# A state-space layer and a routed feed-forward layer in one kernel: one pass instead of two for the last 42 inner units of the down product

## The chip, the cores and the metric

The kernel runs on one core of a Trainium2 chip. A core has a matrix engine (TensorE, PE in the profile; its weight loads are PEld), VectorE (DVE), ScalarE (ACT), GpSimd (POOL) and SyncE (SP), each with its own stream of instructions, which meet by semaphores. The metric is the time of one execution on the device in microseconds (us).

## What is computed

There are 4096 tokens (2 sequences of 2048) of width 256. First comes a diagonal state-space layer with residual and layer norm, and then a feed-forward layer over the result `x`:

```python
gate = x @ Wg.T + routing_bias                      # 8 experts, the best 4 per token
weights = softmax(gate where chosen) * chosen
out = swiglu(x, Ws1, Ws2, Ws3)                      # the shared expert, every token
for e in 8 experts:                                 # H = 682 inner units
    out += weights[:, e] * swiglu(x, W1[e], W2[e], W3[e])
y = layernorm(x + out)
# swiglu(u, w1, w2, w3) = (silu(u @ w1.T) * (u @ w2.T)) @ w3.T
```

Everything is float32. The products of the feed-forward layer are made in float16 with both factors split into a high and a low half: high x high + high x low + low x high.

## The kernel before

**Stages.** Eight steps of 512 tokens make the state-space layer (0 to 120 us; the first shared block lies among them). Then come shared blocks of 256 tokens each, nine ahead of the experts and seven behind them. Meanwhile GpSimd scatters every token's row to its four experts' places (`scatter`, lines 618 to 627: 4 x 32 indirect DMAs, `pad_rows` after each of the first three). The eight experts run over their rows in full blocks of 256 rows and at most one half block of 128 at an expert's end (`expert_blocks`): here 63 full and 6 half ones. With the 16 shared blocks that makes 79 full and 6 half blocks. At the end the experts' rows are gathered and added (`gather`, line 670), and the last layer norm is made lot by lot in the tail (`finish`, from line 1319, on VectorE, after the low parts of the block that was just run).

**A block.** The 682 inner units are 5 whole chunks of 128 and a last chunk (c = FC = 5) of REM = 42. TensorE makes `up` (line 921: 6 matmuls for each of the 11 column sets, 66 of them) into `psA`. For each chunk ScalarE makes the silu (764), VectorE multiplies (`gated`, 1241), ScalarE rounds to the high half (`high`, 770), and VectorE subtracts for the low half (`low`, 1250). TensorE then makes `down` (lines 944 and 949), chunk by chunk, each after a wait for its low half, and after the last chunk's matmuls the outputs are scaled and stored by ScalarE (796) or added by VectorE (1268). `up` takes the chunks in order too, so silu and the halves of the last chunk lie beside `down` of the first ones.

**The last chunk.** Its high half stands in rows 0 to 41 of `g_hi[:, 5]` and its low half in rows 64 to 105 of the same tile. The high half of the weights stands in both places of `w3[..., 0, ...]`; `w3[..., 1, ...]` has the low half of the weights in rows 0 to 63 and zeros below. Two matmuls over 106 rows for each 128 tokens make all the products (line 949): 4 in a full block, 2 in a half one.

**Weights.** Two sets for the experts lie in `work` (w = e % 2), one for the shared expert in `wshared`. All arrive as float32 in `stage` and are split. The shared set is split by ScalarE and VectorE (`shared_high`, `shared_low`), so is the first expert's (`first_high`, `first_low`), and the other seven by GpSimd: `convert_step` runs `high_part` (553, 554) and `low_part` (560, 563) over six pieces. For experts 1 and 2 these steps stand between the scatters of the second and fourth choice (`convert_beside`); for expert 3 the conversion comes after the last scatter and the pad rows (loop from line 684), and those of the later experts after the end of the expert whose set they take. At the end of a conversion `weight_set_ready` is raised (line 588), for which TensorE waits before each expert (`first` in `experts`).

## Time and profile before

| | us |
|---|---|
| runs shown (3) | 1084.09, 1082.38, 1077.70 |
| median | 1082.38 |
| the profiled execution | 1085.63 |
| its span, first to last instruction | 1083.8 |
| TensorE busy | 1009.8 (93%) |
| VectorE busy | 580.3 (54%) |
| ScalarE busy | 502.7 (46%) |
| GpSimd busy | 533.6 (49%) |
| mean granted clock of TensorE | 0.98 of full speed |

Spans and busy times are of the profiled execution. Busy shares are means over stages: what a stage waits for must be read in its timeline. A matmul's own length in the rows is that of its way through the array, where several are at once, so its price is taken from the distance of blocks. In the timeline, "[idle before <- releaser]" is the time in which the engine stood still before the row, and what ended it.

### The profile page before, as it was taken

To read this page: it belongs to the slowest core of one execution; us is meant where nothing else is said; L and a number is where in the kernel's file an instruction comes from. 1 tells how busy PE (TensorE), PEld (TensorE's weight loads), DVE (VectorE), ACT (ScalarE), POOL (GpSimd) and SP (SyncE) were. 2 spreads that over 40 slices of the span, in tenths; PEclk is the share of its full clock that TensorE was granted. 3 is DMA by queue.
4 is the path that set the end of the run, shared out by engine and by line. 5 is a ranking of instruction groups with operands and counts; after the bars stand their busy time and mean duration, and the time that the engine had idled before them with its cause. 6 is when DMAs were issued, how large, how long until landed. Compare 5 with 4: busy or idle time off the path is not lost.

```text
span 1083.8 us, 27280 instructions
## 1 busy us (share of the span) xinstructions
PE 1009.8 (93%) x8784; PEld 857.8 (79%) x8785; DVE 580.3 (54%) x1584; ACT 502.7 (46%) x1282; POOL 533.6 (49%) x486
## 2 busy tenths in 40 slices
PE   7897989988999999999989999999999999999984
PEld 3455878876888888788878878878888888888864
DVE  3898885545444345644545344444345444344676
ACT  2555554432444444444444444544444444454454
POOL 3465135358233337623664006065678674676761
PEclk9998999998999999999999999999999999999998
DMA  7855223432532333253244223127763764866673
GB/s 223 200 137 117 59 70 96 141 93 75 167 99 86 94 94 99 84 162 95 56 132 126 54 49 112 46 53 163 114 103 62 113 104 79 116 101 99 86 141 103
DMA packets 167716, 113.84 MB, mean 105 GB/s; under 512 B 113388, under 2 KB 159983, under 8 KB 166512
## 3 DMA queue, kind: packets, MB, share of 16 engines
q0 software_dynamic: 30480, 59.41, 25.8%
q1 hardware_dynamic: 114944, 32.33, 14.7%
q10 hardware_dynamic: 22240, 21.50, 5.8%
q8 instruction: 21, 0.34, 0.1%
q14 instruction: 31, 0.25, 0.1%
HBM read 47.09 MB, written 40.96 MB: 81 GB/s over the span
## 4 chain that ended last, share of the span: by engine, by line
PE 69%; DMA 10%; DVE 9%; issue 5%; ACT 4%; POOL 1%; SPq 1%; ACTq 1%; DVEq 0%; POOLq 0%
PE psA L921 44%; PE psB L944 17%; DMA rows_by_place<-y_rows,place 4%; PE psB L949 3%; PE psA L872 3%; DMA y_sum<-rows_by_place,place 2%; DVE g_lo L1250 2%; DVE g L1241 1%; PE psC L903 1%; ACT sil L764 1%; DVE stat L1329 1%; ACT y_sum L836 1%; SPq L465 1%; PE psC L896 1%; DMA xb_odd<-rows_by_place 1%
## 5 line engine op out<-in xcount | busy, mean ns | idle before, releaser
L1241 DVE SCALAR_TENSOR_TENSOR g<-psA,sil 128x256 f32<-128x256 f32 (+1 forms) x510 | 207.7, 413 | 442.7 <-ACT sil L764 405.9
L764 ACT ACTIVATE sil<-psA 128x256 f32<-128x256 f32 (+1 forms) x510 | 187.1, 373 | 299.6 <-PE psA L921 224.0
L670 POOL DMA_INDIRECT y_sum<-rows_by_place,place x128 | 199.5, 1559 | 105.7 <-DMA y_sum<-rows_by_place,place 80.3
L921 PE MATMUL psA<-xb,work 128*128 128x256 f16 x2046 | 233.4, 276 | 8.1 <-issue 4.3
L921 PE MATMUL psA<-xb_odd,work 128*128 128x256 f16 x2112 | 235.9, 273 | 4.5 <-DMA xb_odd<-rows_by_place 3.7
L625 POOL DMA_INDIRECT rows_by_place<-y_rows,place x128 | 128.6, 1005 | 225.9 <-DMA rows_by_place<-y_rows,place 180.9
L944 PE MATMUL psB<-work,g_hi 128*128 128x256 f16 x1320 | 222.3, 273 | 11.8 <-DVE g_lo L1250 11.3
L921 PEld LDWEIGHTS psA<-xb,work 128*128 128x128 f16 x2046 | 201.9, 99 | 35.8 <-issue 10.1
L770 ACT ACTIVATE g_hi<-g 128x256 f16<-128x256 f32 (+1 forms) x510 | 206.3, 405 | 51.4 <-DVE g L1241 44.1
L921 PEld LDWEIGHTS psA<-xb_odd,work 128*128 128x128 f16 x2112 | 205.8, 98 | 30.5 <-issue 6.6
L1250 DVE TENSOR_TENSOR g_lo<-g,g_hi 128x256 f16<-128x256 f32 (+1 forms) x425 | 209.2, 492 | 8.7 <-ACT g_hi L770 2.9
L944 PE MATMUL psB<-work,g_lo 128*128 128x256 f16 x660 | 180.4, 273 | 0.0
L944 PEld LDWEIGHTS psB<-work,g_hi 128*128 128x128 f16 x1320 | 126.4, 98 | 34.0 <-DVE g_lo L1250 19.0
L921 PE MATMUL psA<-xb,wshared 128*128 128x256 f16 x1056 | 121.4, 276 | 4.2 <-DVE g L1241 2.9
L921 PEld LDWEIGHTS psA<-xb,wshared 128*128 128x128 f16 x1056 | 104.0, 99 | 18.8 <-DVE g L1241 4.3
L553 POOL TENSOR_SCALAR work<-stage 128x704 f16<-128x704 f32 (+1 forms) x42 | 36.1, 859 | 119.4 <-PE psB L949 109.6
L944 PEld LDWEIGHTS psB<-work,g_lo 128*128 128x128 f16 x660 | 64.7, 98 | 7.6
L872 PE MATMUL psA<-work,sm 128*128 128x512 f32 x128 | 60.6, 624 | 7.3 <-DMA work<-xT 7.3
L560 POOL TENSOR_TENSOR work<-stage,work 128x704 f16<-128x704 f32 (+2 forms) x42 | 63.2, 1505 | 2.9
L944 PE MATMUL psB<-wshared,g_hi 128*128 128x256 f16 x320 | 54.2, 273 | 8.7 <-DVE g_lo L1250 7.3
L796 ACT ACTIVATE eb<-psB,row_weights_odd 128x256 f32<-128x256 f32 x64 | 26.8, 470 | 74.5 <-PE psB L949 58.5
L796 ACT ACTIVATE eb<-psB,row_weights 128x256 f32<-128x256 f32 x62 | 26.0, 470 | 72.7 <-PE psB L949 54.3
(135 smaller groups left out, 709.8 us busy)
## 6 DMA issues: line engine op xcount, KB each, us to landing
stage<-wpack POOLq DMA_DIRECT2D x9, 2176.0 KB, 9.2
rows_by_place<-eb ACTq DMA_DIRECT2D x63, 256.0 KB
work<-xT SPq DMA_DIRECT2D x8, 512.0 KB, 4.9
work<-half_beta SPq DMA_DIRECT2D x8, 512.0 KB, 4.9
work<-x_tok POOLq DMA_DIRECT2D x8, 512.0 KB, 6.0
out<-y_sum ACTq DMA_DIRECT2D x5, 512.0 KB
rows_by_place<-y_rows,place POOLq DMA_INDIRECT x128, 2.5
y_sum<-rows_by_place,place POOLq DMA_INDIRECT x128
```

The costliest lines, as they stand in the source:

```text
L553: t.add(pool.tensor_scalar(parts_of(w, a, m)[0], stage[:, a:a + m], WS, 1.0, ALU.mult, ALU.mult))
L560: t.add(pool.tensor_tensor(lo[:, 0:full], stage[:, a:a + full], hi[:, 0:full], ALU.subtract))
L625: pool.indirect_dma_start(out=xs, out_offset=bass.IndirectOffsetOnAxis(ap=place[:, k, n:n + 1], axis=0), in_=y_rows[:, n, :], in_offset=No ...
L670: pool.indirect_dma_start(out=y_sum[:, n, :], out_offset=None, in_=xs, in_offset=bass.IndirectOffsetOnAxis(ap=place[:, k, n:n + 1], axis=0 ...
L764: act.activation(sil[r0:r0 + n, c % SLOTS, 0:T], psA[0:n, c % HVS, 0:T], ACT.Silu, scale=1.0 / (XS * WS)).then_inc(silu_ready, 1)
L770: act.activation(g_hi[0:n, c, 0:T], g32[0:n, c % SLOTS, 0:T], ACT.Copy).then_inc(gated_high_ready, 1)
L796: last = act.activation(eb[:, j, :], psB[:, j, 0:D], ACT.Copy, scale=row_weights[slot][:, j, e:e + 1])
L872: last = pe.matmul(psA[:, q, :], wdi[:, w, k, m * P:(m + 1) * P], xt[b][:, k, :], start=(k == 0), stop=(k == KD - 1))
L921: last = pe.matmul(dst, W[:, ws, k, ci, :], xb[slot][:, KD * xs_ + k, 0:T], start=(k == 0 and n == 0), stop=(k == KD - 1 and n == 2))
L944: pe.matmul(o, a[:, c, j * P:(j + 1) * P], W3[:, ws, c, :], start=(c == 0 and n == 0), stop=False)
L1241: dve.scalar_tensor_tensor(g32[0:n, c % SLOTS, 0:T], src, 1.0 / (XS * WS), sil[r0:r0 + n, c % SLOTS, 0:T], ALU.mult, ALU.mult).then_inc(ga ...
L1250: dve.tensor_tensor(dst, g32[0:n, c % SLOTS, 0:T], g_hi[0:n, c, 0:T], ALU.subtract)\
```

## The change

The last chunk's down product takes one pass over 128 rows. The 42 units are two parts: Q = 32 units and QV = 10 units.

- `pack` lays the weights so that the up product itself makes three copies of the last 10 units (rows 32 to 41, 42 to 51, 52 to 61). Silu and multiplication run over 64 rows instead of 42.
- `g_hi[:, 5]` then holds: high of the 32 units in rows 0 to 31, low of the 10 in rows 32 to 41, high of the 10 in rows 42 to 61, low of the 32 in rows 64 to 95 and high of the 32 in rows 96 to 127. For this ScalarE makes a second copy (`high_doubled`) and VectorE makes the low half in two instructions.
- `w3[..., 1, ...]` of that chunk holds the high weights in rows 0 to 51 and 64 to 95 (`MIXED`) and the low ones elsewhere. VectorE makes this by a low part over all rows and two copies (shared set, first set); GpSimd by two multiplications with per-row factors (`low_row`, `low_sign`) ahead of one subtraction.
- Three memsets of GpSimd go, eight small ones of VectorE come at the start.

```diff
+    Q = 32
+    QV = REM - Q
+    MIXED = [(0, Q + 2 * QV), (R2, R2 + Q)]
...
-            pool.memset(w3[SH][:, 1, FC * D:DW], 0.0).then_inc(consts_ready, 1)
...
 def low_part(t, w, a, m):
                 t.add(pool.tensor_tensor(lo[:, 0:full], stage[:, a:a + full], hi[:, 0:full], ALU.subtract))
                 if full < m:
+                    t.add(pool.tensor_scalar(stage[:, a + full:a + m], stage[:, a + full:a + m], low_row[:, 0:1], 1.0,
+                                             ALU.mult, ALU.mult))
+                    t.add(pool.tensor_scalar(lo[:, full:m], hi[:, full:m], low_sign[:, 0:1], 1.0,
+                                             ALU.mult, ALU.mult))
                     t.wait()
-                    t.add(pool.tensor_tensor(lo[0:R2, full:m], stage[0:R2, a + full:a + m], hi[0:R2, full:m],
-                                             ALU.subtract))
+                    t.add(pool.tensor_tensor(lo[:, full:m], stage[:, a + full:a + m], lo[:, full:m], ALU.subtract))
...
-            for w in range(2):
-                pool.memset(w3[w][:, 1, FC * D:DW], 0.0).then_inc(sets_cleared, 1)
-            pool.wait_ge(sets_cleared, 2)
+            pool.sem_inc(sets_free, 1)
+            pool.wait_ge(rows_marked, 8)
...
 def silu(c):
-                    n = P if c < FC else REM
+                    n = P if c < FC else R2
...
 def high(c):
-                    n = P if c < FC else REM
+                    n = P if c < FC else R2
                     act.activation(g_hi[0:n, c, 0:T], g32[0:n, c % SLOTS, 0:T], ACT.Copy).then_inc(gated_high_ready, 1)
+                    if c == FC:
+                        act.activation(g_hi[R2 + Q:P, c, 0:T], g32[0:Q, c % SLOTS, 0:T], ACT.Copy)\
+                            .then_inc(high_doubled, 1)
...
 def down(w, g, T=TB):
                     pe.wait_ge(gated_low_ready, NC * g + c + 1 + SLOTS)
+                    if c == FC:
+                        pe.wait_ge(high_doubled, g + 1)
...
-                            r = R2 + REM
-                            for ws in range(2):
-                                last = pe.matmul(o, g_hi[0:r, c, j * P:(j + 1) * P], W3[0:r, ws, c, :],
-                                                 start=False, stop=(ws == 1))
+                            last = pe.matmul(o, g_hi[:, c, j * P:(j + 1) * P], W3[:, 1, c, :], start=False, stop=True)
...
 def shared_low(i):                                  # first_low(i) likewise
-                dve.scalar_tensor_tensor(lo[:, 0:full], stage[:, a:a + full], WS, hi[:, 0:full],
-                                         ALU.mult, ALU.subtract).then_inc(shared_low_ready, 1)
+                dve.scalar_tensor_tensor(lo, stage[:, a:a + m], WS, hi, ALU.mult, ALU.subtract)\
+                    .then_inc(shared_low_ready, 1)
                 if full < m:
-                    dve.scalar_tensor_tensor(lo[0:R2, full:m], stage[0:R2, a + full:a + m], WS, hi[0:R2, full:m],
-                                             ALU.mult, ALU.subtract).then_inc(shared_low_ready, 1)
+                    dve.wait_ge(shared_low_ready, i + 1)
+                    for r, end in MIXED:
+                        dve.tensor_copy(lo[r:end, full:m], hi[r:end, full:m]).then_inc(shared_low_ready, 1)
...
 def gated(c):
-                    r0, n = (0, P) if c < FC else (R2, REM)
-                    src = psA[:, c % HVS, TB:TB + T] if c < FC else psA[R2:R2 + REM, c % HVS, 0:T]
+                    r0, n = (0, P) if c < FC else (R2, R2)
+                    src = psA[:, c % HVS, TB:TB + T] if c < FC else psA[R2:P, c % HVS, 0:T]
...
 def low(c):
                     if c < FC:
-                        dst, n = g_lo[:, c, 0:T], P
+                        rows = [(g_lo[:, c, 0:T], 0, P)]
                     else:
-                        dst, n = g_hi[R2:R2 + REM, c, 0:T], REM
-                    dve.tensor_tensor(dst, g32[0:n, c % SLOTS, 0:T], g_hi[0:n, c, 0:T], ALU.subtract)\
-                        .then_inc(gated_low_ready, 1)
+                        rows = [(g_hi[R2:R2 + Q, c, 0:T], 0, Q), (g_hi[Q:REM, c, 0:T], Q, REM)]
+                    for dst, r, end in rows:
+                        last = dve.tensor_tensor(dst, g32[r:end, c % SLOTS, 0:T], g_hi[r:end, c, 0:T], ALU.subtract)
+                    last.then_inc(gated_low_ready, 1)
```

## Rows read from the trace of the kernel before

**Rows 1.** The page, part 1: busy us, share, instructions of each engine.

```profile
PE 1009.8 (93%) x8784; PEld 857.8 (79%) x8785; DVE 580.3 (54%) x1584; ACT 502.7 (46%) x1282; POOL 533.6 (49%) x486
```

**Rows 2.** Timeline, undisturbed blocks: start, us, engine, line, operation, [idle before].

```profile
507.34 0.42 ACT L770 ACTIVATE g_hi<-g 42x256 f16<-42x256 f32 x1 [0.21 <-DVE g L1241]
...
507.79 0.42 DVE L1250 TENSOR_TENSOR g_hi<-g,g_hi 42x256 f16<-42x256 f32 x1
...
509.33 0.60 PE L949 MATMUL psB<-work,g_hi 106*128 106x256 f16 x4
...
520.25 0.60 PE L949 MATMUL psB<-work,g_hi 106*128 106x256 f16 x4
```

**Rows 3.** Timeline of GpSimd (POOL), scatters, pad rows and conversion, 145 to 531 us.

```profile
145.72 1.15 POOL L625 DMA_INDIRECT rows_by_place<-y_rows,place  x1 [30.18 <-DVE y_rows L1135]
...
528.92 0.98 POOL L613 DMA_INDIRECT rows_by_place<-zeros,pad_at  x1 [1.91 <-DMA rows_by_place<-zeros,pad_at]
530.51 0.77 POOL L553 TENSOR_SCALAR work<-stage 128x704 f16<-128x704 f32 x1 [0.61 <-issue]
```

**Rows 4.** Timeline of GpSimd: one multiplication, and the ends of three conversions.

```profile
8.94 0.43 POOL L567 TENSOR_SCALAR half_beta<-sm 128x256 f32<-128x256 f32 x1
...
266.74 0.99 POOL L625 DMA_INDIRECT rows_by_place<-y_rows,place  x1 [0.82 <-POOL work L563]
...
451.29 0.74 POOL L563 TENSOR_TENSOR work<-stage,work 64x256 f16<-64x256 f32 x1
452.86 0.99 POOL L625 DMA_INDIRECT rows_by_place<-y_rows,place  x1 [0.82 <-DMA rows_by_place<-y_rows,place]
...
549.99 0.66 POOL L563 TENSOR_TENSOR work<-stage,work 64x256 f16<-64x256 f32 x1
551.27 0.63 POOL L550 DMA_DIRECT2D stage<-wpack  x1 [0.62 <-POOL work L563]
```

**Rows 5.** Timeline of TensorE between experts 2 and 3.

```profile
551.19 0.38 PE L949 MATMUL psB<-work,g_hi 106*128 106x256 f16 x2
552.45 3.77 PE L921 MATMUL psA<-xb_odd,work 128*128 128x256 f16 x33 [0.87 <-DMA xb_odd<-rows_by_place]
```

**Rows 6.** By windows, line 949 alone: us, PE busy (count), PEld, clock, DMA.

```profile
0.00:552.00 552.00, 22.93 (x148) 14.21 (x148) 0.98 0.41 111
552.00:985.00 433.00, 23.29 (x152) 14.04 (x152) 1.00 0.51 97
985.00:1084.00 99.00, 4.21 (x28) 2.71 (x28) 0.96 0.59 105
```

**Rows 7.** Timeline of VectorE and TensorE beside GpSimd's conversions.

```profile
243.44 2.10 DVE L1250 TENSOR_TENSOR g_hi<-g,g_hi 42x256 f16<-42x256 f32 x1
245.60 0.61 PE L949 MATMUL psB<-work,g_hi 106*128 106x256 f16 x4 [1.30 <-DVE g_hi L1250]
...
825.86 0.93 DVE L1250 TENSOR_TENSOR g_hi<-g,g_hi 42x256 f16<-42x256 f32 x1
...
826.85 0.61 PE L949 MATMUL psB<-work,g_hi 106*128 106x256 f16 x4
```

**Rows 8.** Timeline of VectorE at the end of a half block.

```profile
359.75 0.28 DVE L1250 TENSOR_TENSOR g_hi<-g,g_hi 42x128 f16<-42x128 f32 x1
```

**Rows 9.** Timeline of TensorE at 649 us, then all engines' busy by windows.

```profile
649.34 9.04 PE L921 MATMUL psA<-xb,work 128*128 128x256 f16 x66 [2.06 <-issue]
...
649.00:654.00 5.00, 4.66 (x28) 3.56 (x29) 0.42 (x1) 0.47 (x2) 4.83 (x6) 0.66 0.14 32
```

**Rows 10.** Timeline of GpSimd: the first gathers of the third and fourth choice.

```profile
915.00 1.54 POOL L670 DMA_INDIRECT y_sum<-rows_by_place,place  x1 [12.33 <-DMA rows_by_place<-eb]
...
988.65 1.54 POOL L670 DMA_INDIRECT y_sum<-rows_by_place,place  x1 [3.98 <-DMA rows_by_place<-eb]
```

**Rows 11.** Timeline of VectorE in the tail.

```profile
1031.41 0.42 DVE L1250 TENSOR_TENSOR g_hi<-g,g_hi 42x256 f16<-42x256 f32 x1
1031.86 2.06 DVE L1329 BATCH_NORM_STATS2 stat<-y_sum 128x6 f32<-128x256 f32 x6
```

More of the change, by code:

```diff
@@ L143, in build @@
         neg_half = sb("neg_half", [P, JT], F32)
+        low_row = sb("low_row", [P, 1], F32)
+        low_sign = sb("low_sign", [P, 1], F32)
         start_state = sb("start_state", [P, 1], F32)
@@ L267, in build @@
         gated_high_ready = sem("gated_high_ready")
+        high_doubled = sem("high_doubled")
         gated_low_ready = sem("gated_low_ready")
@@ L575, in _ @@
                 if s == len(pieces):
-                    pool.wait_ge(shared_low_ready, len(pieces) + 1)
+                    pool.wait_ge(shared_low_ready, len(pieces) + len(MIXED))
                     fetch(1)
@@ L593, in conversion @@
             def conversion(n):
-                return Tally(pool, convert_steps, 3 * len(pieces) + 1, n - 2)
+                return Tally(pool, convert_steps, 3 * len(pieces) + 3, n - 2)
             def convert(n, w):
@@ L646, in _ @@
             pad_rows(0)
-            pool.wait_ge(first_low_ready, len(pieces) + 1)
+            pool.wait_ge(first_low_ready, len(pieces) + len(MIXED))
             fetch(2)
@@ L986, in _ @@
             pe.wait_ge(states_read, 2 * NSTEP)
-            pe.wait_ge(shared_low_ready, len(pieces) + 1)
+            pe.wait_ge(shared_low_ready, len(pieces) + len(MIXED))
             down(SH, 0)
@@ L994, in _ @@
             pe.wait_ge(blocks_ready, 1)
-            pe.wait_ge(first_low_ready, len(pieces) + 1)
+            pe.wait_ge(first_low_ready, len(pieces) + len(MIXED))
             pe.sem_inc(weight_set_ready, 1)
@@ L1004, in _ @@
         def _(dve):
+            for flag, high in ((low_row, 0.0), (low_sign, -1.0)):
+                dve.memset(flag[:, :], high).then_inc(rows_marked, 1)
+            dve.wait_ge(rows_marked, 2)
+            for flag in (low_row, low_sign):
+                dve.memset(flag[Q:R2, :], 1.0).then_inc(rows_marked, 1)
+                dve.memset(flag[R2 + Q:P, :], 1.0).then_inc(rows_marked, 1)
+            dve.wait_ge(rows_marked, 6)
+            for flag, high in ((low_row, 0.0), (low_sign, -1.0)):
+                dve.memset(flag[Q:Q + 2 * QV, :], high).then_inc(rows_marked, 1)
             dve.wait_ge(small_loaded, 16)
@@ L1401, in pack @@
         up[:, :, :, n:2 * FC:2, :] = wt[..., :FC * P].reshape(E1, P, KD, FC, P)
-        up[:, :, :, 2 * FC, n * 64:n * 64 + REM] = wt[..., FC * P:]
+        up[:, :, :, 2 * FC, n * 64:n * 64 + 32] = wt[..., FC * P:FC * P + 32]
+        for r in range(32, 32 + 3 * (REM - 32), REM - 32):
+            up[:, :, :, 2 * FC, n * 64 + r:n * 64 + r + REM - 32] = wt[..., FC * P + 32:]
     down = np.zeros((E1, P, FC + 1, D), W3.dtype)
@@ L1405, in pack @@
     down[:, :, :FC] = w3t[:, :FC * P].reshape(E1, FC, P, D).transpose(0, 2, 1, 3)
-    for n in range(2):
-        down[:, n * 64:n * 64 + REM, FC] = w3t[:, FC * P:]
+    for r in (0, 64, 96):
+        down[:, r:r + 32, FC] = w3t[:, FC * P:FC * P + 32]
+    for r in range(32, 32 + 3 * (REM - 32), REM - 32):
+        down[:, r:r + REM - 32, FC] = w3t[:, FC * P + 32:]
     wpack = np.concatenate([up.reshape(E1, P, -1), down.reshape(E1, P, -1)], axis=2)
```

16 lines of the change are left out of this document (9 added, 7 removed).

## The prediction

> **What bounds the kernel now.** I read the page's busy shares first: TensorE is busy 93% of the span, so at first sight every matmul taken out is time gained [rows 1]. The timeline of one undisturbed block comes next. The end of one block's down product and the end of the next lie 10.92 us apart (509.33 to 520.25) [rows 2], and a block of 256 rows is 100 matmuls of 256 columns: 66 of the up product, 30 of the whole chunks, 4 of the last chunk. One matmul thus costs 10.92 / 100 = 0.109 us of TensorE. (The mean of 273 ns that the groups show is the pipelined length of one, not its price.) The third view is the timeline of GpSimd, because a kernel that is 93% TensorE can still have points where TensorE waits for somebody who doesn't get faster. There is one. From 145.72 to 528.92 us GpSimd issues the scatters and the pad rows one by one, most of them after the landing of an earlier one, and from 530.51 it converts the weights of expert 3 (the fourth) [rows 3]. That conversion ends at 550.65, GpSimd goes on at 551.27, and TensorE, whose last matmuls of expert 2 begin at 551.19, begins expert 3 at 552.45 [rows 4, 5]. Nothing in that chain of GpSimd waits for TensorE. So TensorE reaches expert 3 less than a microsecond from the moment its weights are ready: the kernel has two bounds until 552 us and mostly one after it.
>
> **What goes.** Line 949 issues 148 matmuls before 552 us, 152 between there and 985, and 28 after it, 328 in all [rows 6]; half of them go, 164 x 0.109 = 17.9 us of TensorE. That is 0.22 us for each of 79 full blocks and 0.11 for each of 6 half blocks. The remaining pass reads 128 rows and not 106, as the 96 other matmuls of a block do at the same 0.109, so that costs nothing.
>
> **What comes, in each block.** VectorE makes the low part of the last chunk in two passes instead of one, 0.42 us more; ScalarE copies 32 rows a second time, again 0.42 us, since a pass over 42 rows takes that [rows 2] and the columns stay. In an undisturbed block both have cover: the low pass ends at 508.21 and TensorE first reads its rows at 509.33 [rows 2], 1.1 us later. The second pass leaves 0.7 us, and the earlier end of the down product doesn't touch that, since the saved matmuls lie behind the read. ScalarE's copy runs beside VectorE's first piece. Behind it are queued the scaling of the output rows and the next block's silu, both later than the down product. These blocks gain the full 0.22 us. If that cover were gone, each would lose 0.42.
>
> Where GpSimd converts weights the cover is gone. The pass that takes 0.42 us takes 2.10 at 243.44, and TensorE waited 1.30 us for it; at 825.86 it takes 0.93 and ends 0.06 us before TensorE's matmul [rows 7]. There the new pass is on the path. Its cost lies between 0.42 and 2.10 less the 0.22 gained. I take 0.43, the undisturbed row, since two GpSimd passes seldom hit both pieces. From expert 3 on I count five such blocks (ending at 574, 662, 725, 816 and 827), before it some eight.
>
> The rule here is that VectorE and GpSimd hold a port against each other. The Trainium skill, SBUF — State Buffer, "Who interferes with whom", says that a VectorE instruction with two inputs in SBUF contends with a GpSimd instruction that reads SBUF and that the loser waits for the whole instruction. The added low piece is such an instruction, so by that page it could wait a full GpSimd pass each time; by that rule alone the five blocks would cost what the second rival below gives. The rows agree that the same pass can be 0.42 or 2.10 us.
>
> In a half block the low passes are the path: the last takes 0.28 us and TensorE's two matmuls follow at its end [rows 8]. One more pass, 0.28, less one matmul, 0.11: 0.17 us lost in each.
>
> **What comes on GpSimd.** Each of seven conversions loses a pass over 64 rows x 256 columns and gets one over 128 rows (equal, 0.66 to 0.74 us) and two multiplications of 256 columns. Such a multiplication took 0.43 us at 8.94 [rows 4]. Two are 0.86; I take 0.8, as they follow one another, with 0.6 and 1.1 as ends. The three memsets that leave GpSimd lay at the start and ahead of a wait of 30.18 us [rows 3]: nothing. The eight small memsets of VectorE lie before its first work, nothing either. For the shared set and the first set the low part becomes one longer pass and two copies, a few tenths beside work that waits for TensorE; I take none, with 0.4 as the end.
>
> **How that chain moves.** The scatters' start comes after the ranks, which VectorE counts right after block 1's low passes: one pass more, 0.42, less the 0.22 that TensorE gave in block 0: +0.2 us. The conversion for expert 1 ends with a scatter that waited for the conversion's own last pass, so +0.8 passes on whole; that for expert 2 ends with one that waited for a landing, 0.82 us after the pass, so between 0 and +0.8, I take 0.7, as the hand-over after the pass costs up to 0.6 (551.27 is that far behind 550.65) [rows 4]. The conversion for expert 3 adds 0.8 in full. Together the weights are ready 2.5 us later. Before, TensorE's start lay up to 0.9 us behind the release (of its 0.87 us of idle I can't tell how much is branching) [rows 5]. So expert 3 starts 1.6 us **later**, ends 0.5 and 2.5. What 27 full blocks saved before it, 27 x 0.22 = 5.9 less about 3.8 for the disturbed and half blocks, becomes a wait of 4 to 5 us at this point.
>
> A stall costs more than itself. After 2.06 us idle at 649.34 behind a half block, 66 matmuls took 9.04 us, in a stretch at a granted clock of 0.66 of full speed, part of it at 1.2 GHz [rows 9]; at the full clock 66 of them are 66 x 0.109 = 7.2, with the lead of the first 7.4. I take +1.7 us for the new stall, ends 0 and 3.4.
>
> **After expert 3.** 152 matmuls of line 949 are 36 full and 4 half blocks [rows 6]: 36 x 0.22 = -7.9; five disturbed blocks +2.2; 4 half blocks 4 x 0.17 = +0.7. GpSimd can't hold this back: it waited 12.33 us for expert 6's rows and 3.98 us for expert 7's [rows 10]; the first loses some 6 to the gain and the two added conversions' 1.6, the second 1.3.
>
> **The tail.** From 988.65 the last gathers and then VectorE's statistics set the pace, and TensorE's saving there is off the path. The statistics start 0.03 us behind the low pass (1031.41, 1031.86) [rows 11]. That occurs in four lots, +0.42 each; the last block gives back the 0.22 of its matmuls: +1.4 us.
>
> **Sum** against the profiled execution, 1085.63 us (1083.8 of span and 1.8 around it): +1.6 + 1.7 - 7.9 + 2.2 + 0.7 + 1.4 = -0.3, so 1085.3. The median of the runs shown is 1082.38, 3.25 below that execution: **1082.1 us**.
>
> **Rivals.**
> First, the scatter chain doesn't hold TensorE: its landings differ from run to run, and it comes some microseconds earlier in most. For it: the margin at 552 is under a microsecond, and single waits in the chain are several microseconds. Against it: it has to win the 2.5 us that it loses and about 2 of TensorE's more. Then the terms are +0.2 at the start, -5.9 + 8 x 0.43 + 2 x 0.17 before expert 3 and -7.9 + 2.2 + 0.7 + 1.4 after: -1.9 - 3.6 = -5.5, 1076.9 us. With cheap disturbed blocks it is up to 5 us less. Chance 0.24.
>
> Second, slower: VectorE's added pass waits for GpSimd's passes. At 2.10 instead of 0.43 in the five blocks that is +8.3, and with one more fall of the clock +1.7: 1082.1 + 10.0 = 1092 us. It decides from the point where such a pass costs more than 1.5 us on the mean. For it is the row at 243.44; against it the row at 825.86. Chance 0.14.
>
> Third, the change doesn't do what it says: TensorE waits for the last chunk in undisturbed blocks too, so that the matmuls saved come back as waiting in every block and the time is the second rival's or more. The 0.7 us of cover speaks against it. Chance 0.02.
>
> **How the numbers follow.** The forecast has 0.60. Its own ends from the bounds: 1076 (no clock fall, no disturbed block, early release) to 1088. The range takes in the first rival and leaves out most of the second: 1074 to 1088. What a measurement of this kernel can tell from no change is 0.5%, 5.4 us. The forecast lies wholly in it but for its edges, the first rival just beyond it: faster 0.25, same 0.60, slower 0.15.
>
> **What would show it.** In the profile after: line 949 with 164 matmuls; undisturbed blocks 10.70 us apart; VectorE's low group of the last chunk twice as often at 0.42 us; the conversion for expert 3 ending near 553 and TensorE idle 4 to 5 us before that expert, at a start of 553 to 555; a lower granted clock just behind it. Wrong if expert 3 starts before 551, if the disturbed blocks lengthen by over a microsecond each, or if undisturbed blocks stay at 10.92.

## The result, and the profile after

The changed kernel takes 1097.53 us (median of 4 runs, 1093.58 to 1102.79) against 1083.24 us for the kernel before on the same chip: a ratio of 1.0131, 95% interval 1.0091 to 1.0172. It is 14 us slower. The forecast was no change, 1082.1 us, in a range of 1074 to 1088; what came is its second rival, which had given 1092 us and a chance of 0.14, and 5 us more than it gave. The profiled execution has a span of 1094.5 us against 1083.8, so the rest of this section accounts for 10.7 us of the 14.

The page after, part 1 (the counterpart of [rows 1]) and the first two groups that matter here, from the list of groups with forms kept apart: engine, line, operation, output and inputs, count, then busy us and mean ns, then the idle time just before and who ended it.

```profile
PE 996.1 (91%) x8620; PEld 837.4 (77%) x8621; DVE 625.0 (57%) x1679; ACT 536.6 (49%) x1367; POOL 542.4 (50%) x497
```

```profile
L1273 DVE TENSOR_TENSOR g_hi<-g,g_hi 10x256 f16<-10x256 f32 x79 | 40.2, 509 | 1.1
L1273 DVE TENSOR_TENSOR g_hi<-g,g_hi 32x256 f16<-32x256 f32 x79 | 38.2, 484 | 2.5
...
L961 PE MATMUL psB<-work,g_hi 128*128 128x256 f16 x132 | 26.0, 275 | 14.9 <-DVE g_hi L1273 14.2
```

The same view of the kernel before:

```profile
L949 PE MATMUL psB<-work,g_hi 106*128 106x256 f16 x264 | 40.8, 275 | 1.6 <-DVE g_hi L1250 1.3
L1250 DVE TENSOR_TENSOR g_hi<-g,g_hi 42x256 f16<-42x256 f32 x79 | 39.7, 502 | 2.5
```

TensorE did lose its 164 matmuls and 14 us of busy time. But read the last field: over the whole run the experts' last-chunk matmuls waited 1.3 us for VectorE's low half before, and 14.2 us after. That is 12.9 us of new waiting, against the 17.9 us that the matmuls were worth. VectorE's single group of 39.7 us became two of 38.2 and 40.2: a piece of 10 rows costs as much as one of 32 or of 42. All three have 256 columns, and half the columns took less (0.28 us for 42 rows by 128, [rows 8]).

**Undisturbed blocks** came out as worked out. Timeline of the changed kernel, VectorE's two pieces and TensorE's matmuls of two blocks that follow each other (the counterpart of [rows 2]):

```profile
510.01 0.84 DVE L1273 TENSOR_TENSOR g_hi<-g,g_hi 32x256 f16<-32x256 f32 x2
...
520.72 0.85 DVE L1273 TENSOR_TENSOR g_hi<-g,g_hi 32x256 f16<-32x256 f32 x2
...
511.53 0.38 PE L961 MATMUL psB<-work,g_hi 128*128 128x256 f16 x2
...
522.26 0.38 PE L961 MATMUL psB<-work,g_hi 128*128 128x256 f16 x2
```

From 511.53 to 522.26 is 10.73 us, most others are 10.70, and the two pieces end (510.01 + 0.84 = 510.85) 0.7 us before they are read. The cover was there in these blocks.

**Where expert 3 begins.** Timeline of TensorE, then of GpSimd at the end of the conversion (the counterparts of [rows 5] and [rows 3, 4]), then busy time by windows (length, PE, PEld, DVE, ACT, POOL with counts, granted clock, DMA share, GB/s):

```profile
541.45 0.61 PE L958 MATMUL psB<-work,g_hi 128*128 128x256 f16 x2 [1.10 <-DVE g_lo L1273]
...
544.60 0.40 PE L961 MATMUL psB<-work,g_hi 128*128 128x256 f16 x1 [1.55 <-DVE g_hi L1273]
553.52 9.45 PE L933 MATMUL psA<-xb_odd,work 128*128 128x256 f16 x66 [8.52 <-issue]
```

```profile
529.67 0.98 POOL L622 DMA_INDIRECT rows_by_place<-zeros,pad_at  x1 [1.91 <-DMA rows_by_place<-zeros,pad_at]
...
550.56 0.48 POOL L569 TENSOR_SCALAR stage<-stage,low_row 128x256 f32<-128x256 f32 x1
551.02 0.48 POOL L571 TENSOR_SCALAR work<-work,low_sign 128x256 f16<-128x256 f16 x1
551.58 0.67 POOL L574 TENSOR_TENSOR work<-stage,work 128x256 f16<-128x256 f32 x1
552.88 0.63 POOL L556 DMA_DIRECT2D stage<-wpack  x1 [0.63 <-POOL work L574]
```

```profile
541.00:544.50 3.50, 1.60 (x6) 0.56 (x6) 3.39 (x5) 0.62 (x2) 3.42 (x5) 0.50 0.18 37
544.00:557.00 13.00, 3.88 (x18) 2.60 (x19) 0.68 (x2) 0.86 (x2) 8.62 (x11) 0.50 0.27 86
```

TensorE begins its last matmuls of expert 2 at 544.60, 6.6 us earlier than before, and then stands for 8.52 us. The view names no releaser ("issue"), but the conversion of expert 3's weights ends in that time, at 552.25, and expert 3 starts 0.64 us behind GpSimd's next fetch (552.88). In the other four profiled kernels with a wait of 6 us or more at this place that distance is 0.61 to 0.65 us too. The gain of the first half is gone there: expert 3 starts 1.07 us later than in the kernel before (553.52 and 552.45). The granted clock is down as well: 0.50 of full speed through the whole window, which is 1.2 GHz, and the first 66 matmuls take 9.45 us where 66 at 2.4 GHz take 7.38. It had fallen before the long wait began: it is 0.50 from 541 on, in the half block that waits several times for VectorE's low halves, and the two matmuls at 541.45 take 0.61 us for the usual 0.39.

**Beside GpSimd's conversions.** The first block of expert 3, all three engines, in the timeline (the counterpart of [rows 7]):

```profile
565.44 0.95 POOL L560 TENSOR_SCALAR stage<-stage 128x704 f32<-128x704 f32 x1
565.78 2.53 DVE L1273 TENSOR_TENSOR g_hi<-g,g_hi 32x256 f16<-32x256 f32 x2
566.47 1.56 POOL L566 TENSOR_TENSOR work<-stage,work 128x704 f16<-128x704 f32 x1
568.37 0.39 PE L961 MATMUL psB<-work,g_hi 128*128 128x256 f16 x2 [1.73 <-DVE g_hi L1273]
```

The view of line 1273 alone splits the pair (minimum, median, maximum in ns):

```profile
L1273 DVE TENSOR_TENSOR g_hi<-g,g_hi x2: 875/1257/1639, 565.8 to 566.7; 32x256 f16<-32x256 f32 x1, 10x256 f16<-10x256 f32 x1
```

The first piece took 0.88 us and the second, begun at 566.7, took 1.64 us in place of 0.42: it ends 0.3 us behind GpSimd's 1.56-us subtraction, which had begun 0.2 us before it. The first piece, too, had started inside a GpSimd pass (565.44 to 566.39) and ended 0.3 us behind it. TensorE waited 1.73 us. From here on there are six such blocks, with waits of 1.73, 1.09, 1.79, 1.73, 1.73 and 1.36 us (at 568.37, 580.63, 667.79, 732.12, 824.55 and 837.08), 9.43 us together. In all six both pieces were held: the first took 0.87 to 1.63 us, the second 0.89 to 1.64, and each of the twelve ended 0.26 to 0.28 us behind the GpSimd pass that it had started in. In the kernel before the single piece was held in the same way in the six blocks from expert 3 on, 0.87 to 0.93 us in five of them and 1.62 in one, and that passed almost without a wait. The Trainium skill, SBUF — State Buffer, "Who interferes with whom", says that a VectorE instruction with two inputs in SBUF contends with a GpSimd instruction that reads SBUF, and that the lock is exclusive. The trace agrees on VectorE's side, by the twelve pieces.

**The account of the difference**, in us, after less before, from the start of the last matmuls of each block (the span itself differs by 10.7, 0.3 of this is given back behind them):

| stretch | difference |
|---|---|
| up to expert 2's last matmuls | -6.6 |
| from expert 2's last matmuls to expert 3's first (8.92 for 1.26) | +7.7 |
| first 66 matmuls of expert 3 (9.45 for 7.38) | +2.1 |
| rest of that block, its wait of 1.73 in it | +2.3 |
| six other blocks whose length changed: 39, 47, 53, 59, 61, 62 | +6.9 |
| all other blocks up to 992 | -4.2 |
| first block of the tail, a fall of the clock in it | +1.7 |
| the other tail blocks | +1.1 |
| sum | +11.0 |

Blocks are numbered from 0 by the order of their down products. In the row of six, block 59 is no wait: behind an idle time of 2.02 us at 788.67 the clock fell and 66 matmuls took 9.04 us, which the kernel before did in 7.38. The fall at [rows 9] is gone in return, which is why block 47, with a wait of 1.79 us, is only 0.1 us longer.

### The profile page after: what moved, and what is told of

The parts are those of the page before. It is cut to its first block, busy times and chain, and to the rows that moved or that the text cites. A ratio compares the mean times of both kernels' runs of the same rounds, so it can differ in the third digit from the quotient of the medians.

```text
span 1094.5 us, 27229 instructions
## 1 busy us (share of the span) xinstructions
PE 996.1 (91%) x8620; PEld 837.4 (77%) x8621; DVE 625.0 (57%) x1679; ACT 536.6 (49%) x1367; POOL 542.4 (50%) x497
## 3 DMA queue, kind: packets, MB, share of 16 engines
q1 hardware_dynamic: 114944, 32.33, 14.8%
## 4 chain that ended last, share of the span: by engine, by line
PE 39%; DMA 30%; POOL 9%; issue 8%; DVE 8%; ACT 3%; SPq 1%; ACTq 1%; DVEq 0%; POOLq 0%
PE psA L933 25%; DMA rows_by_place<-y_rows,place 22%; PE psB L958 8%; DMA y_sum<-rows_by_place,place 3%; POOL rows_by_place L634 3%; POOL work L566 2%; PE psA L884 2%; DMA rows_by_place<-zeros,pad_at 2%; POOL work L559 1%; POOL stage L560 1%; PE psC L915 1%; DVE g L1263 1%; DVE g_hi L1273 1%; ACT sil L773 1%; DVE g_lo L1273 1%
## 5 line engine op out<-in xcount | busy, mean ns | idle before, releaser
L933 PE MATMUL psA<-xb,work 128*128 128x256 f16 x2046 | 230.3, 274 | 10.5 <-issue 5.8
L933 PEld LDWEIGHTS psA<-xb,work 128*128 128x128 f16 x2046 | 199.2, 98 | 38.2 <-issue 13.4
L1273 DVE TENSOR_TENSOR g_hi<-g,g_hi 32x256 f16<-32x256 f32 (+2 forms) x170 | 83.6, 492 | 3.9
```

Source lines behind the costliest of these rows:

```text
L933: last = pe.matmul(dst, W[:, ws, k, ci, :], xb[slot][:, KD * xs_ + k, 0:T], start=(k == 0 and n == 0), stop=(k == KD - 1 and n == 2))
L1273: last = dve.tensor_tensor(dst, g32[r:end, c % SLOTS, 0:T], g_hi[r:end, c, 0:T], ALU.subtract)
```

## The experiments

Theory after this reading, **D**: most of the loss is VectorE's second piece, which waits behind whole GpSimd passes wherever weights are converted. Rival **W**: the weights of expert 3 come too late from GpSimd, and the rest follows from that stall. A third, **S**: the matmuls weren't worth their price. All times are medians; the ratio is to the kernel before on the same chip, whose own median moved between 1080.9 and 1083.3 us from one set of runs to the next.

### The second VectorE piece alone, in the kernel before

```diff
-                        dst, n = g_hi[R2:R2 + REM, c, 0:T], REM
-                    dve.tensor_tensor(dst, g32[0:n, c % SLOTS, 0:T], g_hi[0:n, c, 0:T], ALU.subtract)\
-                        .then_inc(gated_low_ready, 1)
+                        rows = [(g_hi[R2:R2 + 32, c, 0:T], 0, 32), (g_hi[R2 + 32:R2 + REM, c, 0:T], 32, REM)]
+                    for dst, r, end in rows:
+                        last = dve.tensor_tensor(dst, g32[r:end, c % SLOTS, 0:T], g_hi[r:end, c, 0:T], ALU.subtract)
+                    last.then_inc(gated_low_ready, 1)
```

> The kernel before with the low half of the last chunk made in two VectorE instructions (rows 0 to 31 and 32 to 41), all else as before: the cost of the added pass by itself. Theory D (beside GpSimd's conversions the second piece waits out a GpSimd pass): 5 blocks after 552 us lose 1 to 1.8 us each, the tail 1.4, so 7 to 11 us slower than before; undisturbed blocks stay at 10.92. Rival (the forecast's price of 0.43 a disturbed block): 3 to 4 us slower. A third: waits before 552 us push expert 3's start as well, then over 11.

Measured: 1095.51 us, ratio 1.0121, interval 1.0083 to 1.0160. One VectorE instruction of 0.42 us more per block, with nothing else changed, costs 12 us. The undisturbed blocks stay at 10.92. Its group of last-chunk matmuls:

```profile
L949 PE MATMUL psB<-work,g_hi 106*128 106x256 f16 x264 | 41.0, 276 | 11.4 <-DVE g_hi L1251 10.5
```

10.5 us of waiting for the low half in place of 1.3. It is over the upper end of theory D's 7 to 11 and fits the third expectation: blocks 10, 11, 35 and 36 wait too (1.85, 0.46, 0.99 and 1.18 us), and expert 3 starts at 554.97, 2.5 us later than in the kernel before. The cost of the piece alone is nearly as large as the whole result of the change, which has the saving in it besides. GpSimd was early in this execution (its next fetch behind the conversion for expert 3 is at 545.80, and TensorE waits 1.84 us for rows, not weights), so W has no part in it. D holds.

### The changed kernel without the second piece

This kernel leaves out the low half of the last 10 units, so its result is not the full one. ScalarE's second copy stays.

```diff
-                        rows = [(g_hi[R2:R2 + Q, c, 0:T], 0, Q), (g_hi[Q:REM, c, 0:T], Q, REM)]
+                        rows = [(g_hi[R2:R2 + Q, c, 0:T], 0, Q)]
```

> The changed kernel without the second VectorE piece (the low half of the last 10 units is left out). Theory D: the waits of TensorE for the last chunk's low half (9.4 us after expert 3's start in the changed kernel) fall under 2 us, so 6 to 9 us faster than the changed kernel; the wait ahead of expert 3 stays at 8 us or more. Rival (the waits come from ScalarE's second copy): no change.

Measured: 1080.53 us, ratio 0.9970, interval 0.9939 to 1.0000: 17 us below the changed kernel where 6 to 9 were expected. The expectation had only the waits behind expert 3's start. Of the 15.4 us between the two profiles, 7.9 lie in the six blocks that had waited there, 3.5 in the two blocks where the clock had fallen, 1.4 in the last four blocks, 1.2 ahead of expert 3, and the rest in half blocks and small pieces. From its groups and its timeline:

```profile
L961 PE MATMUL psB<-work,g_hi 128*128 128x256 f16 x132 | 25.7, 273 | 1.2 <-DVE g_hi L1273 0.9
```

```profile
552.32 9.29 PE L933 MATMUL psA<-xb_odd,work 128*128 128x256 f16 x66 [10.97 <-issue]
...
782.51 7.38 PE L933 MATMUL psA<-xb,work 128*128 128x256 f16 x66 [1.69 <-issue]
...
981.52 7.38 PE L933 MATMUL psA<-xb,wshared 128*128 128x256 f16 x66 [1.55 <-SPq L425]
```

The waits for the low half are gone (0.9 us in all), and with them the two late falls of the clock: behind 1.69 and 1.55 us of idle 66 matmuls take 7.38 us, where the changed kernel took 9.04 in both places. But that the second piece brings these falls isn't shown, and other kernels speak against it: the piece alone, above, has neither, and the saving alone with the pad rows moved, below, which has no second piece, has the later one (9.04 us from 975.58 on, behind 1.74 us of idle). With the waits gone while ScalarE's second copy is still made, the rival that the copy causes them is out. W's stall is still there, longer even, 10.97 us: TensorE arrives earlier at a gate that doesn't move. So both are real, D is the dear one, and the gate swallows what is gained before it.

### The saving alone

This kernel leaves out the product of the high halves with the low parts of the weights for the last 42 units. All other engines do what they did.

```diff
-                            for ws in range(2):
-                                last = pe.matmul(o, g_hi[0:r, c, j * P:(j + 1) * P], W3[0:r, ws, c, :],
-                                                 start=False, stop=(ws == 1))
+                            last = pe.matmul(o, g_hi[0:r, c, j * P:(j + 1) * P], W3[0:r, 0, c, :],
+                                              start=False, stop=True)
```

> The kernel before with the second of the last chunk's two matmul passes taken out of the down product: high and low halves of the last 42 units still meet the first set of weight rows, but not the second, so the product of high halves with the low parts of the weights is left out for these 42 units. VectorE, ScalarE and GpSimd do exactly what they did: the saving alone. If the saving is worth what the prediction's term says wherever TensorE is not waiting (0.22 us per full block, 0.22 x 36 = 7.9 after expert 3's start, and nothing before it, since expert 3's weights end the wait there): 1075 to 1078 us, with the idle time before expert 3 at 5 to 8 us in place of 0.9, and waits for VectorE's low half where they were, none over 1.3 us. If the same clock falls come that the changed kernel has (a longer wait at expert 3, one more fall near 785): 1078 to 1082. If the shorter block lets other engines end it (waits in undisturbed blocks): clean blocks above 10.75 and a time at or above 1082.

Measured: 1074.87 us, ratio 0.9934, interval 0.9902 to 0.9967. The forecast of 1075 to 1078 was met at its lower edge, and S is out: clean blocks are 10.70 us and the saving is worth 6.0 us by the medians (1080.89 for the kernel before) and 7.1 by the ratio, close to the 7.9 of the prediction's term for the blocks behind the gate. The timeline of TensorE shows the gate again:

```profile
545.54 10.00 PE L921 MATMUL psA<-xb_odd,work 128*128 128x256 f16 x66 [6.05 <-issue]
```

Even with no work added anywhere the whole gain of the first half ends in a wait of 6.05 us, and the clock with it (10.00 us for 66 matmuls). Six or seven microseconds is all that the dropped pass could bring as the kernel stood.

### The gate moved: the pad rows behind the conversion

The pad rows of experts 4 to 7 stood between the scatters and the conversion for expert 3, and nobody needs them so early. Here GpSimd issues them after that conversion, first in the changed kernel, then in the kernel before.

```diff
-            for e in range(3, E):
-                pool.wait_ge(pads_written[e - 1], 16)
-                pad_rows(e)
+            pool.wait_ge(pads_written[2], 16)
+            pad_rows(3)
...
+                    if e == 1:
+                        for later in range(4, E):
+                            pool.wait_ge(pads_written[later - 1], 16)
+                            pad_rows(later)
```

> The changed kernel, with the pad rows of experts 4 to 7 issued after the conversion of expert 3's weights instead of ahead of it, so that the conversion starts some 12 us earlier. Theory W (TensorE, now early, waits 8.5 us for these weights and then runs at 1.2 GHz for 4 us): expert 3 starts at 545 to 547 us instead of 553.5, no wait over 1.5 us ahead of it and no fall of the clock behind it; 8 to 10 us faster than the changed kernel, about 1088. Rival P (the added VectorE pass is all of the loss and the wait at expert 3 only hides slack that is lost again later): within 3 us of the changed kernel.

> The kernel before with the same move of the pad rows. Theory W: TensorE reached expert 3 at about the moment its weights were ready, so it gains nothing, 1081 to 1085 us. Rival: there too TensorE had been held back; then it is over 3 us faster.

Measured: 1089.97 us for the changed kernel (ratio 1.0055, interval 1.0016 to 1.0094), 7.6 us less than unmoved, close to the 8 to 10 expected. The stall is gone and no fall of the clock follows it, as the timeline of TensorE shows at the start of expert 3:

```profile
552.43 1.81 PE L936 MATMUL psA<-xb_odd,work 128*128 128x256 f16 x15 [0.99 <-DMA xb_odd<-rows_by_place]
```

But expert 3 starts at 552.43 and not at 545 to 547: TensorE now arrives late by itself. Two of the blocks that stand beside the moved conversion (34 and 35) take 12.95 and 13.30 us, with waits of 1.73 and 1.43 us for the low half, where the unmoved kernel has 10.70 and 10.74. Part of what the gate had cost is paid there. There are 12.2 us of waits for the low half in that profile, so the second piece can account for what remains above the kernel before.

The kernel before with the same move: 1075.88 us, ratio 0.9929, interval 0.9896 to 0.9961. Here 1081 to 1085 was expected and the gain of 7.4 us is larger. [rows 5] show a wait of only 0.87 us at the gate, which was the reason to expect little. What it misses is in the next fence. It has the timeline of TensorE in two executions of this same program (the second from a later run of it, below): the starts of expert 3.

```profile
550.70 7.38 PE L924 MATMUL psA<-xb_odd,work 128*128 128x256 f16 x66 [0.89 <-DMA xb_odd<-rows_by_place]
```

```profile
540.15 7.38 PE L924 MATMUL psA<-xb_odd,work 128*128 128x256 f16 x66 [1.87 <-DMA row_weights_odd<-rows_by_place]
```

With the gate out of the way (GpSimd's next fetch is at 533.86 in the one and 530.16 in the other) expert 3 starts at 540 in one profile and at 551 in the other. The difference lies in the blocks beside the conversions before expert 3: the blocks ending at 233, 247 and 259 us in the one took 16.6, 13.4 and 12.9 us, in the other 12.4, 13.4 and 13.2; the block that ends at 449 and at 441 took 15.1 and 12.6. The profiled execution of the kernel before was a late one (14.8 and 17.8 us for two of these blocks). The times go with it: 1083.88 and 1072.87 us for these two executions, 1085.63 for the late one of the kernel before. In an early one, I take it, TensorE stands at the gate for microseconds; there is no profile of an early one of the kernel before. One profile showed a margin of under a microsecond, and it was one draw of two quantities that each move by several microseconds or more.

### The change mended, step by step

First a layout of rows in which the low halves of all 42 units lie side by side, so that VectorE makes them in one instruction. It has to wait for ScalarE's second copy, which now covers rows that it overwrites. The full result.

```diff
-    MIXED = [(0, Q + 2 * QV), (R2, R2 + Q)]
+    MIXED = [(0, REM), (R2, R2 + REM)]
...
-                        rows = [(g_hi[R2:R2 + Q, c, 0:T], 0, Q), (g_hi[Q:REM, c, 0:T], Q, REM)]
+                        dve.wait_ge(high_doubled, g + 1)
+                        rows = [(g_hi[R2:R2 + REM, c, 0:T], 0, REM)]
```

> The changed kernel with its last chunk's rows laid out anew: rows 0 to 63 hold high halves (42 units, then copies of 22), rows 64 to 105 low halves of all 42 units, rows 106 to 127 high copies of the remaining 20. VectorE makes the low halves in one pass, as the kernel before did, but it waits for ScalarE's second copy first. The full result. If VectorE's second pass behind GpSimd is the main loss: as the experiment without that pass, 1079 to 1085, clean blocks 10.70, idle before expert 3 9 to 11 us, waits for the low half under 0.9 us in all but one or two blocks, and no added clock fall near 785 and 990. If the loss lies in the length of the chain (high, copy, low) and not in the count of VectorE's passes: the copy now stands ahead of the pass, so waits of 1 to 2 us stay and the time is 1093 to 1100.

Measured: 1088.55 us, ratio 1.0059, interval 1.0025 to 1.0093. It falls between the two expectations. The waits for the low half are 3.7 us in place of 14.2, as D would have it. But expert 3 begins only at 555.24, behind 7.75 us of idle: in this execution GpSimd ended its conversion 1.7 us later still.

Then the two added multiplications of GpSimd are taken out. The high tile of the last chunk is multiplied by a factor that is the scale or zero by rows, so that the subtraction itself leaves the mixed tile:

```diff
+                    t.add(pool.tensor_scalar(hi[:, full:m], stage[:, a + full:a + m], low_row[:, 0:1], 1.0,
+                                             ALU.mult, ALU.mult))
...
-                    t.add(pool.tensor_scalar(stage[:, a + full:a + m], stage[:, a + full:a + m], low_row[:, 0:1], 1.0,
-                                             ALU.mult, ALU.mult))
-                    t.add(pool.tensor_scalar(lo[:, full:m], hi[:, full:m], low_sign[:, 0:1], 1.0,
-                                             ALU.mult, ALU.mult))
```

> The experiment with the new layout of rows, and with GpSimd's conversion shortened: the two added multiplications of the last chunk's weights are gone (the high tile is multiplied by a per-row factor of the scale or zero instead, so that the subtraction gives the mixed tile). Their 12 chunk steps of two added passes at 0.47 to 0.75 us go; one pass of the high tile is split in two. If expert 3's weights on GpSimd are what TensorE waits for, the conversion is 2 to 4 us shorter, the wait before expert 3 falls by as much against the experiment with the new layout alone (to 6 to 9 us), and the time is 1 to 4 us below it, 1077 to 1082. If GpSimd's added multiplications are hidden, the two times are equal within 1 us.

Measured: 1083.07 us, ratio 1.0021, interval 0.9994 to 1.0048: 5.5 us below the layout alone, more than the 1 to 4 expected. Expert 3 begins at 548.81, behind 6.09 us of idle. The interval takes in 1: this version can't be told from the kernel before. So GpSimd's passes seem not to be hidden. I can't say that all 5.5 us are theirs: the start moved by 6.4 us, of which two passes of 0.48 in each of three conversions explain 3 at most, and the end of that chain differed by microseconds between kernels with equal GpSimd work (the fetch behind it came at 551.27 in the kernel before and at 544.92 with the saving alone).

At last the pad rows are moved as well:

> As the experiment before it, and the pad rows of experts 4 to 7 are issued by GpSimd after the conversion for expert 3. All three causes are away: VectorE's second pass, the two multiplications, and the pad rows ahead of the conversion. If they add up: the wait of 6 to 9 us before expert 3 falls to 1 to 2 us and its clock fall (1.7 to 2.1 us) with it, against some 2 to 3 us that the blocks beside the moved conversion lose: 1068 to 1074 us, ratio to the kernel before 0.985 to 0.992. If moving the pad rows only moves GpSimd's disturbance on to other blocks: 1075 to 1081, no better than the kernel before with its pad rows moved (1075.9).

Measured: 1070.78 us, ratio 0.9909, interval 0.9881 to 0.9938, inside the band for "they add up". This version has the full result and is faster than both kernels. What it doesn't tell is whether the change has a part in that, since the moved pad rows alone gave 0.9929.

### Three kernels with the pad rows moved, side by side

The saving alone, the kernel before, and the mended change, all with the moved pad rows:

> The saving alone (the kernel before, the second matmul pass of the last 42 units left out, that is the product of their high halves with the low parts of the weights) and the pad rows of experts 4 to 7 issued after the conversion for expert 3. The most that the dropped pass can give. The saving alone was 1074.9 with 6 us of waiting before expert 3 and the pad rows moved gave 7 us by themselves. If the wait is what ate the saving of the first half: no wait above 1.2 us before expert 3, and 1062 to 1068 us, ratio 0.981 to 0.987. If the two gains are the same one: 1071 to 1075.

> The kernel before with the pad rows of experts 4 to 7 moved behind the conversion for expert 3, a second time, beside its two companions. It was 1075.9 us, ratio 0.993: expected again 1073 to 1079, ratio 0.990 to 0.996.

> The mended change with the pad rows moved, a second time, beside its two companions. If the mended change is worth something of its own: 1068 to 1073 us, and 3 to 7 us less than the kernel before with its pad rows moved. If it is not: within 2 us of it. Against the saving alone with pad rows moved it is longer by its tail (0.43 us in each of the last four blocks, 1.7) and by the blocks with a wait for the low half, in all 3 to 7 us.

Measured: the saving alone 1065.93 us, ratio 0.9841 (0.9798 to 0.9884), with 0.95 us of idle before expert 3, so the wait was what ate the saving of the first half; the kernel before 1073.07, ratio 0.9932 (0.9900 to 0.9964); the mended change 1074.12, ratio 0.9934 (0.9903 to 0.9966). With the gate gone, the dropped pass is worth 7 us more than moving the pad rows (1073.07 less 1065.93). The 3 to 7 us expected between the mended change and the kernel before weren't there; it keeps nothing of this that can be measured: over the two measurements it stands at 0.991 and 0.993, the kernel before with moved pad rows at 0.993 and 0.993. The gain of this whole study is the move of the pad rows.

Where the 7 us went can be read from the profiled executions of the last two. The mended change is 1.7 us ahead at the end of block 12 and 3.5 at that of block 26 (413 us). It loses 2.6 in blocks 27 to 29, beside the second conversion, and 2.1 each in blocks 33 and 59 (14.81 and 14.61 us long, for 12.70 and 12.48). In each of these two the granted clock fell, and 66 matmuls took 9.04 us for 7.38, which is 3.3 of the 4.2 us. It is 3.0 ahead again at 1002 us and 1.1 at the end, since the last four blocks cost it 0.43 to 0.58 more each. Its waits for the low half add up to 5.4 us, against 0.2 in the other kernel:

```profile
L968 PE MATMUL psB<-work,g_hi 128*128 128x256 f16 x132 | 25.8, 274 | 5.7 <-DVE g_hi L1271 5.4
```

```profile
L952 PE MATMUL psB<-work,g_hi 106*128 106x256 f16 x264 | 40.3, 272 | 0.5 <-DVE g_hi L1253 0.2
```

So three things took the 7 us in this pair of profiles: waits for the low half, two falls of the clock and the tail. VectorE's pass starts 0.42 us later there, behind the copy; that it met GpSimd more often for this reason is likely and not shown.

## Why the prediction was wrong

**The step that failed** is the price of VectorE's second piece beside the conversions: "I take 0.43, the undisturbed row, since two GpSimd passes seldom hit both pieces". The bounds were right (0.42 to 2.10; the second piece took 0.89 to 1.64) and the choice between them was not. The six blocks behind expert 3's start waited 9.43 us, 1.6 each, where the term had 2.2 in all for five. (The sixth was there to be counted: in the kernel before the pass at 561.42 took 0.88 us.) What failed is "seldom hit both pieces": both were held in all six blocks. GpSimd's cycle on a slab of 704 columns is three passes that fill it without a gap (0.95, 1.56 and 0.95 us from 565.44 on), so an instruction of VectorE nearly always starts inside one of them and waits for its end, and the next instruction then starts inside the next pass. Even the row at 825.86 [rows 7], which the prediction read as nearly free, was such a wait: 0.93 us for 0.42, held by a multiplication of 0.99 that ended at 826.51. In the kernel before one wait of that size fitted into the cover of 1.1 us. Two in a row don't, and in five of the six blocks one of the two passes met was the subtraction (1.20 to 1.57 us). The second rival named this, with its point of decision, "more than 1.5 us on the mean", and it was passed. The experiment with the piece alone, 12 us, and the one without it, 17 us the other way, show it as the cause of most of the loss. They don't add up to the result, though: 12 less the 6 or 7 of the saving leaves 8 to 9 of the 14 us to the rest of the change. Moving the pad rows gave back 7.6 of it, and leaving out GpSimd's two multiplications 5.5 in the other layout; how these overlap is open.

**The clock**: one fall at expert 3 was counted, +1.7, and measured +2.1; it began in the half block ahead of the stall, not behind it. Two more came, at 788.67 and 993.86, 1.7 each (9.04 for 7.38), and one behind a half block went (7.38 us at 655.30 for 9.04 at 649.34 before). They were left out of the sum and stood only in the rival, as one. What brings them is open: without the second piece neither came, but neither came with the second piece alone. Two more were in the kernel before and not in the changed one, here by windows of the kernel before:

```profile
246.00:251.00 5.00, 4.69 (x28) 3.40 (x27) 0.42 (x1) 1.22 (x3) 4.58 (x6) 0.66 0.33 108
260.00:268.00 8.00, 6.82 (x38) 4.75 (x39) 3.35 (x4) 1.64 (x4) 6.59 (x7) 0.57 0.20 68
```

The changed kernel has 1.00 from 238 to 268 us.

**The wait before expert 3** was foreseen in kind. "Starts 1.6 later" was 1.07; the conversion grew by 0.5 us and not 0.8 (531.58 to 552.25, for 530.51 to 550.65), since the two multiplications take 0.46 a step, the longer subtraction no more than the short one (0.67 and 0.66), and the other passes ran 0.4 shorter in all. "A wait of 4 to 5 us" was 8.52. TensorE came earlier than worked out, -6.6 us at the end of expert 2, since the blocks ending at 241 and 254 us took 12.5 and 12.3 us, for 14.8 and 17.8, the second with the clock down. Whether that is the change or the draw isn't shown. The kernel before with moved pad rows has 12.9 to 13.4 us in the same two blocks in both its profiles, but in one of them 16.6 in the block ahead. Blocks 9 to 11 together took 39.0 to 47.7 us in the six profiles of the kernel before and its variants, and 36.9 to 40.8 in six of the seven of the changed kernel and its variants (43.9 in the one without the second piece). Little hung on it, as the gate absorbs it.

**The undisturbed blocks** were right: 10.70 us, 0.22 gained, the cover of 0.7 us measured as 0.7. Ten of them took 10.82 to 10.91 instead, with no wait shown (the rows have the next block's first up matmul 0.15 us late). In nine of these ten the kernel without the second piece and the one with the saving alone have 10.70, and in eight the mended ones have 10.87 to 10.97. So it goes with the later end of the low half, and the cover was short there by a wait that I hadn't seen; on what that matmul waits is open. With 0.18 each it is under 2 us. The -7.9 of the term was for 36 full blocks. Of these, 29 stand in the row of -4.2 in the account, where they would be -6.4: six of the ten just named cost 1.1 of that, and five others, which follow a disturbed or a half block, kept their length, 1.1 more. The four half blocks, +0.7 in the forecast, came out even.

**The tail**: +1.4 was forecast; its blocks take 14.43, 13.27, 15.03 and 13.26 us for 14.07, 12.83, 14.67 and 12.83, +1.6 in all. The two blocks ahead of them gained 0.22 each, which the term had off the path, so the tail without the fall of the clock cost 1.1. Right in mechanism and near in size; the first block of the tail brought the fall of the clock.

**The first rival**, the chain of scatters that doesn't hold TensorE, was not what happened, but its reason, "its landings differ from run to run", was right and mattered more than I gave it. The end of the conversion for expert 3 can be read from the next fetch of GpSimd: 551.27 before, 552.88 after, but 554.59 with the new layout and 544.92 with the saving alone, whose GpSimd work is that of the kernel before. A sum around this gate from a single profile, good to a microsecond, had no ground. The range of 14 us was made of the bounds of my own terms, and it left out most of a rival that needed nothing but the value at the end of a row I had quoted.

## What to carry to other kernels

Where a short instruction has been seen to wait for another engine's long passes, price it at the long pass and not at its own length, each piece of it, until a run shows otherwise; split in two, each piece can wait for a pass of its own, as in all six blocks here, even where its time alone is covered. Before you credit a saving, look for a gate behind it that doesn't move, and look in more than one execution, since the margin at a gate is the difference of two times that both vary. And test the parts by themselves: the saving alone and the added instruction alone gave 6 or 7 and 12 us, and with them the sign.

## What the runs showed of the hardware

- VectorE's time here doesn't depend on the rows: 10, 32 and 42 rows of 256 columns take the same 0.42 us undisturbed, 0.48 to 0.51 on the mean of the run.
- The same small two-input pass of VectorE takes 0.42 us alone and 1.64 beside a GpSimd subtraction of 1.56 us; the pair of 0.84 takes 2.53 (565.78).
- GpSimd, too, is slower beside VectorE: the multiplication by a factor of each row, 128 rows by 256 columns, took 0.48 us at 550.56, while VectorE stood, and 0.74 at 453.44 in this group of the changed kernel's timeline:

```profile
453.44 0.74 POOL L569 TENSOR_SCALAR stage<-stage,low_row 128x256 f32<-128x256 f32 x1
454.17 0.61 POOL L571 TENSOR_SCALAR work<-work,low_sign 128x256 f16<-128x256 f16 x1
```

- The length of an idle time doesn't tell whether TensorE's clock falls behind it. In the changed kernel 2.02 us of idle at 788.67 was followed by a fall (9.04 us for 66 matmuls), while 2.12 us at 655.30 was not (7.38). Ahead of the same block 59, 2.07 us was followed by a fall in the mended kernel with moved pad rows (767.13) and by none in the one with the new layout alone (787.03). What else it depends on isn't shown. The changed kernel's two rows:

```profile
655.30 7.38 PE L933 MATMUL psA<-xb,work 128*128 128x256 f16 x66 [2.12 <-DMA row_weights<-rows_by_place]
...
788.67 9.04 PE L933 MATMUL psA<-xb,work 128*128 128x256 f16 x66 [2.02 <-issue]
```
